# Counting of edges: edge units dealt over 24 of 25 blocks instead of the first five heavily, two queues written out

## The reference, cut to what matters

```
x[idx].add over edges:  segment_sum(feat[src] * w, dst)   # hops: a dense matrix of edge counts is used
deg_col = segment_sum(ones, dst)                          # degrees
edge_feat = relu(edge_attr @ W_edge + b_edge)             # 100000 x 96
mu = mean(h, axis=0); var = mean(square(h - mu), axis=0)  # over all edges
```

## Time and profile before

| | us |
|---|---|
| median of 3 runs | 2815.41 (2802.81, 2816.22, 2815.41) |
| profiled execution | 2801.42 |
| its span, first to last instruction | 2799.7 |
| the changed stage in that span | about 52.7 to 601 |

### The profile page before, as it was taken

The page is one execution under the profiler, slowest core; times in us unless marked ns, Lnnn a source line. Parts: engine busy times, 40 slices in busy tenths (PEclk is TensorE's granted clock), DMA queues, the critical chain, the costliest instruction groups (busy, mean ns, idle before and its releaser), DMA issues. The chain is left out here.

```text
span 2799.7 us, 50246 instructions
## 1 busy us (share of the span) xinstructions
PE 1853.1 (66%) x14611; PEld 1446.8 (52%) x14611; DVE 1564.5 (56%) x4031; ACT 861.7 (31%) x1484; POOL 936.1 (33%) x1182
## 2 busy tenths in 40 slices
PE   1777777779999999778525544544555555555488
PEld 0333444459999999745413433333444344333477
DVE  7856866665444444465434555555555555555753
ACT  1687566641111111121212222222222222222420
POOL 3311211131000000000166666666666666666100
PEclk9988988879999999889755555555555555555699
DMA  4211111110000000800132222222222222222200
GB/s 138 93 49 41 42 70 56 70 63 2 2 2 2 2 2 2 311 1 3 37 44 49 49 49 48 47 49 48 50 50 49 49 50 49 49 48 48 69 1 18
DMA packets 86652, 133.19 MB, mean 48 GB/s; under 512 B 48616, under 2 KB 55656, under 8 KB 86462
## 3 DMA queue, kind: packets, MB, share of 16 engines
q1 hardware_dynamic: 40398, 83.53, 8.8%
q0 software_dynamic: 25344, 38.98, 6.9%
q10 hardware_dynamic: 20720, 8.06, 1.3%
HBM read 95.89 MB, written 34.58 MB: 47 GB/s over the span
## 5 line engine op out<-in xcount | busy, mean ns | idle before, releaser
L1430 POOL DMA_INDIRECT counts<-p_rows,rows x784 | 745.6, 951 | 498.4 <-issue 224.0
L931 PE MATMUL ps_hop<-y,counts 128*128 128x192 f16 x6250 | 525.0, 247 | 21.6 <-DVEq L818 12.3
L1659 PE MATMUL ps_e_z<-e_w_q,counts 128*128 128x96 f32 x1568 | 364.1, 427 | 259.8 <-ACT counts L1595 219.9
L931 PEld LDWEIGHTS ps_hop<-y,counts 128*128 128x128 f16 x6250 | 520.0, 98 | 26.5 <-DVEq L818 12.4
L1659 PEld LDWEIGHTS ps_e_z<-e_w_q,counts 128*128 128x128 f32 x1568 | 341.8, 330 | 295.8 <-ACT counts L1595 249.9
L560 DVE TENSOR_TENSOR hot_w<-iota_w,places_now 128x1600 f16<-128x1600 f16 x300 | 297.0, 990 | 156.0 <-PE ps_counts L586 137.1
L586 PE MATMUL ps_counts<-hot_w,hot_p 128*128 x1196 | 287.6, 372 | 117.5 <-DVE hot_p L560 77.4
L1670 PE MATMUL ps_e_seg<-counts 128*128 128x192 f16 x784 | 140.7, 359 | 301.9 <-DVE counts L1470 151.1
L1670 PEld LDWEIGHTS ps_e_seg<-counts 128*128 128x128 f16 x784 | 100.4, 138 | 385.3 <-issue 198.2
L1595 ACT ACTIVATE counts<-ps_e_u 96x1024 f32<-96x1024 f32 x98 | 99.9, 1019 | 642.0 <-remote 591.1
L527 POOL TENSOR_TENSOR places_now<-places,origins (+1 forms) x302 | 115.4, 383 | 428.0 <-DVE hot_p L560 278.3
(11 more groups left out here) (401 smaller groups left out, 2483.4 us busy)
## 6 DMA issues: line engine op xcount, KB each, us to landing
counts<-count_rows SPq DMA_DIRECT2D x30, 800.0 KB, 6.6
count_rows<-attr_split SPq DMA_DIRECT2D x25, 800.0 KB, 3.8
counts<-p_rows,rows POOLq DMA_INDIRECT x784
e_attr<-attr_parts SPq DMA_DIRECT2D x99, 72.0 KB
attr_parts<-attr_split SPq DMA_DIRECT2D x9, 784.0 KB, 15.9
attr<-attr_parts SPq DMA_DIRECT2D x50, 140.6 KB
e_dst_rows<-dst_row SPq DMA_DIRECT2D x99, 64.0 KB
e_w_q<-q_rows ACTq DMA_DIRECT2D x392, 12.0 KB
```

The lines of the kernel that those rows point to most:

```text
L931: mm = pe.matmul(ps[:, r, 0:2 * D], k.counts[:, m, b, :], y[:, odd, b, :], start=b == 0, stop=b == NB - 1)
L1430: nc.gpsimd.indirect_dma_start(z[:, slot, j, :], None, k.p_rows, bass.IndirectOffsetOnAxis(rows, 0)) \
L1659: mm = pe.matmul(ps_z[:, two, j // (STEP_TILES // 2), at:at + D], u_hot[:, two, j * P:(j + 1) * P], w_q[:, fed, j // Q_TILES, :], start=Tr ...
```

## The change

The units are dealt out in another way, and both loops are gone. Before, blocks 0 to 4 had 7, 7, 6, 5 and 5 units, blocks 5 to 24 one each. Now blocks 0 to 8 have 7, 5, 5, 4, 4, 3, 3, 2 and 2, blocks 9 to 23 one each, and block 24 none. A table `PLACES` gives the windows behind which they stand: five at 0, 2, 3, 5, 7; four at 0, 2, 4, 6; three at 0, 3, 6; two at 1, 5; one at 2 (as before). ACT's rule is changed too: in blocks with one or two units, the rectifying comes one window behind the products (as before for one unit) and the squares two windows behind (before: three); in blocks with three or more both follow at once.

```diff
-    EARLY = [7, 7, 6, 5, 5]
+    UNITS = [7, 5, 5, 4, 4, 3, 3, 2, 2] + [1] * (NB - 10) + [0]
+    PLACES = {1: (2,), 2: (1, 5), 3: (0, 3, 6), 4: (0, 2, 4, 6), 5: (0, 2, 3, 5, 7), 7: (1, 2, 3, 4, 5, 6, 7), 0: ()}
...
         def units_of(d):
 
-            early = len(EARLY)
-            if isinstance(d, int) and d < early:
-                first = sum(EARLY[0:d])
-                return [(first + n, n + (d == 0)) for n in range(EARLY[d])]
-            return [(d + (sum(EARLY) - early), 2)]
-
-        def for_blocks(eng, one_block):
-
-            early = len(EARLY)
-            for d in range(early):
-                one_block(d, d % 2)
-            with eng.Fori(0, (NB - early) // 2) as two:
-                for odd in (1, 0):
-                    one_block(two * 2 + (early + 1 - odd), odd)
+            first = sum(UNITS[0:d])
+            return [(first + n, at) for n, at in enumerate(PLACES[UNITS[d]])]
...
-            for_blocks(sp, one_block)
+            for d in range(NB):
+                one_block(d, d % 2)
...
                     for n, at in units:
-                        if len(units) > 1 and j == at:
+                        if len(units) > 2 and j == at:
                             rectified(n)
                             squares(n)
-                        elif len(units) == 1 and j == at + 1:
+                        elif len(units) <= 2 and j == at + 1:
                             rectified(n)
-                        elif len(units) == 1 and j == at + 3:
+                        elif len(units) <= 2 and j == at + 2:
                             squares(n)
 
-            for_blocks(act, one_block)
+            for d in range(NB):
+                one_block(d, d % 2)
```

More of the change, by code:

```diff
@@ L418, in count_edges @@
     PARTS = [(0, 7), (7, 13), (13, 19), (19, NB)]
-    EARLY = [7, 7, 6, 5, 5]
-    assert sum(EARLY) + NB - len(EARLY) == U_UNITS and len(EARLY) % 2 == 1
+    UNITS = [7, 5, 5, 4, 4, 3, 3, 2, 2] + [1] * (NB - 10) + [0]
+    PLACES = {1: (2,), 2: (1, 5), 3: (0, 3, 6), 4: (0, 2, 4, 6), 5: (0, 2, 3, 5, 7), 7: (1, 2, 3, 4, 5, 6, 7), 0: ()}
+    assert sum(UNITS) == U_UNITS and len(UNITS) == NB
     DEGREE = BANK - 64
@@ L480, in load @@
                 sp.dma_start(attr[0:PRODUCTS, :],
-                             k.attr_parts[:, bass.ds(n * (U_PARTS * U_EDGES), U_PARTS * U_EDGES)]).then_inc(attr_in, 16)
+                             k.attr_parts[:, n * (U_PARTS * U_EDGES):(n + 1) * (U_PARTS * U_EDGES)]).then_inc(attr_in, 16)
             def one_block(d, odd):
                 for n, _ in units_of(d):
-                    if not isinstance(n, int) or n:
+                    if n:
                         sp.wait_ge(u_done, n)
@@ L490, in one_block @@
                 sp.wait_ge(window_out, d * WINDOWS + (WINDOWS + 2))
-                sp.dma_start(k.count_rows[bass.ds(d, 1), :, :].rearrange("a p e -> (a p) e"),
+                sp.dma_start(k.count_rows[d, :, :],
                              staged[:, odd, :, :].rearrange("p b s -> p (b s)")).then_inc(counts_stored[odd], 16)
@@ L664, in turn @@
                 act.wait_ge(turned, d * len(PARTS) + (n + 1))
-                out = nc.scalar.copy(k.counts[:, lo:hi, bass.ds(d, 1), :].rearrange("p b a s -> p b (a s)"),
+                out = nc.scalar.copy(k.counts[:, lo:hi, d, :],
                                      turned_in(n % 2, hi - lo))
                 if n == len(PARTS) - 1:
-                    out = nc.scalar.activation(k.deg_in[:, bass.ds(d, 1)], ps_t[:, n % 2, DEGREE:DEGREE + 1], ACT.Copy,
+                    out = nc.scalar.activation(k.deg_in[:, d:d + 1], ps_t[:, n % 2, DEGREE:DEGREE + 1], ACT.Copy,
                                                scale=2.0)
@@ L673, in rectified @@
                 act.wait_ge(u_done, n + 1)
-                if not isinstance(n, int) or n:
+                if n:
                     act.wait_ge(u_summed, n)
                 nc.scalar.activation(u[:, :, :], ps_u[:, :, 0:U_EDGES], ACT.Relu,
-                                     accum_out=u_sums[:, 0, bass.ds(n, 1)]).then_inc(u_taken, 1)
+                                     accum_out=u_sums[:, 0, n:n + 1]).then_inc(u_taken, 1)
             def squares(n):
@@ L681, in squares @@
                 nc.scalar.activation(u[:, :, :], u[:, :, :], ACT.Square,
-                                     accum_out=u_sums[:, 1, bass.ds(n, 1)]).then_inc(u_summed, 1)
+                                     accum_out=u_sums[:, 1, n:n + 1]).then_inc(u_summed, 1)
             def one_block(d, odd):
@@ L687, in one_block @@
                     window(d, odd, j)
-                    if j % 2 == 0 and not (isinstance(d, int) and d == 0):
+                    if j % 2 == 0 and d:
                         turn(d - 1, j // 2)
                     for n, at in units:
-                        if len(units) > 1 and j == at:
+                        if len(units) > 2 and j == at:
                             rectified(n)
                             squares(n)
-                        elif len(units) == 1 and j == at + 1:
+                        elif len(units) <= 2 and j == at + 1:
                             rectified(n)
-                        elif len(units) == 1 and j == at + 3:
+                        elif len(units) <= 2 and j == at + 2:
                             squares(n)
-            for_blocks(act, one_block)
+            for d in range(NB):
+                one_block(d, d % 2)
             for n in range(len(PARTS)):
```

## The result

| | before | changed kernel |
|---|---|---|
| median of 17 runs | 2811.71 us (2802.81 to 2817.18) | 2819.51 us (2812.19 to 2825.11) |
| ratio, with 95% interval | | 1.0028 [1.0019, 1.0037] |
| profiled execution | 2801.42 us | 2821.73 us |

The change made the kernel slower, by 0.28%: the interval does not reach 1, but the difference is within the 0.5% that I had taken as "the same". The forecast was 2826 us and slower.

What follows compares the result with a forecast made beforehand. ACT bounds blocks 1 to 4, mostly DVE 5 to 8, PE's serial queue 9 to 24. -20.9 + 16.5 + 21.7 - 1.5 + 0 = +15.8 us: 2817.2 from the profiled execution, 2831.2 from the median; 2826 taken, range 2792 to 2846.

Steps and rivals of the forecast that it cites:

- Part 1: Blocks 0 to 4: fewer units, spread over the windows, gain 20.9 us; bounds about 12 and 33.
- Part 2: Blocks 5 to 8: more units, with PE waiting for loads at heads, lose 16.5 us; bounds 4 and 24.
- rival 3: Heads of blocks 5 to 8 cost little and squares nothing, as PE makes up its stops: -18.4 us; chance 0.12.
- Part 3: Blocks 9 to 23: squares one window earlier delay PE's opening, 1.45 us a block, 21.7 lost; bounds 0 and 28.
- rival 1: Late blocks: PE's later gaps take up the squares' 1.45 us, so the sum is -5.9 us; chance 0.17.
- Rival 2: Late blocks: PE's new wait makes the clock fall more often, total +28 us, 2829 to 2843; chance 0.14.
- Part 4: Block 24 without a unit: PE loses 1.04 us of work and a wait, gain 1.5 us; bounds 1.0 and 3.
- Part 5: Loops written out: register instructions already pass while ACT works, so 0 us; bounds 4 gained and 4 lost.

Runs made afterwards that it cites:

- before_again: The kernel before, unchanged, profiled once more: 2807.2 us, ratio 1.0 [0.9986, 1.0013].
- heads_shifted: Changed kernel with units of three-, four- and five-unit blocks moved off window 0, TensorE's loop number shifted by 5 and masked: ratio 1.0028 to the kernel before.
- after_sq3: Changed kernel with the squares of one-unit blocks put back to three windows behind the products: 2804.3 us, ratio 0.9981 to the kernel before.
- before_sq2: Kernel before with only the squares of one-unit blocks moved, two windows behind the products instead of three: 2827.0 us, ratio 1.0061.
- before_flat: Kernel before with only the loops of SyncE and ScalarE written out for all 25 blocks: 2814.3 us, ratio 1.0023.
- heads_masked: Changed kernel with units moved off window 0, the batch number masked by one more operation per batch on PE and GpSimd: 2854.5 us, ratio 1.0129 to before.

## Why the prediction was right, and where its numbers were off

The direction was right, and so were the mechanisms of the gain (fewer units in the early blocks) and of both losses (heads, squares). That the total lies near the forecast is partly luck: three sizes were off by 6 to 9 us each, and a part of their errors cancels.

- **Part 1** (-20.9): right. T 4.7 came 20.8 us earlier. By block, T to T, forecast 32.4, 28.6, 28.0, 30.1, measured 32.2, 28.1, 26.9, 30.4: 22.4 us gained in blocks 1 to 4, less 1.6 in block 0, which was longer for no reason of the change (123.3 in before_again too).
- **Part 2** (+16.5): right in kind, a little high. Blocks 5 to 8 took 30.0, 27.9, 24.6 and 19.4 us, 14.0 more than before's 87.9; forecast 30.2, 29.1, 23.7 and 21.4. The mechanism is shown by heads_shifted: there PE waits 2.3 us for `attr` in all instead of 19.1, and block 5 with three units takes 25.4 us, 1.2 more than before with one (at a clock of 1.00 against 0.88). So rival 3's premise, that PE makes up its stops, failed.
- **Part 3** (+21.7): the mechanism is right, the size holds for the window and not for the total. Window 6 grew by 1.39 us against 1.45, whichever way the edit was made, so rival 1 is out. But the squares put back took 13 us off the total (8 to 18 by the two intervals), 0.9 us for each of 15 blocks; the squares moved alone put 17 on (13 to 22), 1.1 for each of 16, where 16 x 1.45 = 23.2. What failed is "behind the opening PE's queue has the same work as before": the same work, but at another clock. I forecast blocks of 16.1 us in the fast clock; not one had it. All of blocks 10 to 23 took 16.8 to 17.2 us at a granted 0.80. Before's late blocks are of several kinds: some have no low clock, some a short stretch (a granted 0.88), and three of 15 in one execution, eight in the other, a long one (0.70) that takes in window 3 with the edge products, 3.94 us against 2.12. In the changed kernel the stretch lies in windows 0 to 2, and window 3 is 2.21. That this is what gives back a part of the 1.39 us is my reading of the windows; no run holds the clock fixed.
- **Rival 2**: its sign came, low clock in every late block, and its loss did not. In blocks 9 to 23 the clock was low for 99 us in the changed kernel and 92 in after_sq3; for 102 in before_sq2, and 65 and 92 in the two executions of before. The new wait made the low stretches regular more than it added to them.
- **Part 4** (-1.5): 0.3, outside its bounds. Block 24 took 14.3 instead of 14.6 us: windows 3 to 5 took 1.0 us less (4.14 against 5.12), windows 0 to 2, in the low clock here, 0.6 more (6.76 against 6.19).
- **Part 5** (0, bounds 4 each way): wrong. Writing the loops out costs 6 us (3 to 10), 0.3 to 0.4 in window 1 of each late block. The failed step is that the loads are "issued up to 0.6 us sooner behind the store, ahead of need", with nothing else reckoned: PE's register load behind SyncE's store and load takes 1.2 us instead of 0.9. The working never asked what the two DMAs do to PE's own sequencer.
- **The sum and its base**: the 15.8 us agree with the 16.3 between the two profiled executions at T 24.7, and that is partly luck: before's, at 2801.4, is lower than all 17 timed runs, with an unusually fast clock in its late blocks. Against before_again it is 9.3, and between the medians 7.8. By the ratios these 8 us are: units dealt out anew (parts 1, 2 and 4) -0.42%, or -12 us (-6 to -18) against the -5.9 forecast (at T 8.7 after_sq3 is 13.4 us ahead of before_flat, the changed kernel only 6.7 ahead of before); squares moved +0.47%, or +13 against 21.7; loops written out +0.23%, or +6 against 0. The two costs together are 2 us under the forecast's, the gain is 6 us over it. From the median of 17 runs, 2811.7, the forecast's sum would give 2827.5; the measured is 8.0 lower.
- **Slips in the working**: in part 2 the terms up to PE's arrival add up to 8.3 and not 8.2; in part 3 the squares would start at 595.13 and the sum goes on from 595.08; in rival 2, 15.8 and half of 21 make 26 and not 28. None changes the outcome.

Open: why the register load takes 0.3 us more when SyncE's loop is written out. Two things change there: the load of `attr` follows the store after 0.39 us, and SyncE issues both without register arithmetic. Against the first, as a matter of degree: in before the load follows after 0.61 us in even blocks and 1.00 in odd ones, and the register load takes 0.9 us in both. A kernel that only delays the load was not run, nor was ScalarE's loop written out alone.

## What to carry to other kernels

Where two engines pass a pair of buffers between them, count what stands ahead of the copy-out in the in-order queue: 1.9 us of side work moved by one place cost 1.4 us in one window of each of 15 blocks, about 1 us a block in the total, while the same move in blocks 5 to 8, behind DVE's pace, was free. A unit placed right behind a queue barrier (here a store that waits for the last drain) pays the whole load latency; one window later it pays next to none. Where a queue's loop reads its limits from memory, look for these reads in the sequencer's rows before you call a gap unexplained. Before adding microseconds to a profiled execution, profile the kernel twice: this one differs from itself by 7 us, as much as the change made.

## What the runs showed of the hardware that I had not expected

- The granted clock moves with the blocks. In the changed kernel 13 of 15 late blocks take 17.0 to 17.2 us, each with one stretch at 1.2 and one at 2.4 GHz, block after block; in heads_masked most take about 17.3 or about 20.2. And it counts where in a block the low stretch falls: in before, block 10 at a granted 0.88 took 14.6 us, as long as block 11 at 1.00, while the blocks at 0.70 took 17.1 and 17.2.
- One register operation more ahead of PE's wait for a batch (heads_masked against heads_shifted) cost 0.07 us in window 2 at the low clock (1.75 against 1.68) and 0.10 in window 7 at the high one (1.94 against 1.84), and the block went from 17.69 to 18.45 us, with 156 us of low clock in blocks 9 to 23 against 126.
- Writing out SyncE's loop, with no work on PE changed, made PE's window 1 0.3 to 0.5 us longer. The register load of PE's sequencer there takes 1.2 to 1.3 us instead of 0.9; away from the store and load it takes 0.30.
